# First attention of a two-layer block: the loads of stacks, values and output weight issued from ScalarE's queue in place of SyncE's

## The chip, the cores and the metric

One Trainium2 chip, one of its cores. The metric is the device time of one execution of the whole kernel in microseconds, the median of several executions. The core has TensorE (PE, matmuls), VectorE (DVE), ScalarE (ACT), GpSimd (POOL) and SyncE (SP); SP and ACT can both issue DMAs, each from a queue of its own. Each engine runs its own program in order and meets the others at semaphores.

## The reference, cut to what matters

Two transformer layers in fp32: x of 2 x 1024 x 512, each layer an attention and a feed forward, each wrapped as x + layernorm(f(layernorm(x))). The change concerns the first attention alone: 16 heads of width 32 per batch entry, rotary embedding, causal softmax.

```python
q, k, v = (proj(Wq), proj(Wk), proj(Wv))
q = q * cos + rotate_half(q) * sin
k = k * cos + rotate_half(k) * sin
scores = jnp.einsum('bhqd,bhkd->bhqk', q, k) / math.sqrt(HD)
scores = jnp.where(causal, -jnp.inf, scores)
attn = jax.nn.softmax(scores, axis=-1)
out = jnp.einsum('bhqk,bhkd->bhqd', attn, v)
```

## The kernel before, in words

The kernel runs phase after phase, with all engines meeting between them. `front_layer0` (before this phase) writes the rotated queries and keys of all heads, split into a high and a low part, and the values to DRAM. `attention_layer0` (L761) then works through 32 heads (16 per batch entry). For each head it holds

- a stack of queries and one of keys in SBUF, `q_stack` and `k_stack`, 96 rows by 1024 positions: the high part twice and the low part once against high, high and low, so that one matmul gives the product of the split numbers. Four such stacks (`STACKS`, L710) are kept in turn. `load_stack(h)` (L796) brings one in with four DMAs (L801 to L804);
- two more rows of the q stack, the negated maximum of every query's scores, in a high and a low part, against rows of ones in the k stack: the matmul of the scores then subtracts the maximum by itself. Those maxima are first computed from a matmul pass of their own;
- the values of a group of four heads (`GROUP_HEADS`), `v_stage`, 33 columns a head with a column of ones that gives the softmax sum. `load_values(group)` (L806) brings them in with one DMA (L811), two groups in turn.

The order of work is written out by `steps_layer0` (L733) as a sequence that every engine walks: i counts units, six to a head (`UNITS`: two for the first half of the queries, four for the second). At step i there is, in this order: at the first unit of a head the transpose of the next head's maxima ("N", L903, split by VectorE at L977 and L979); the scores of unit i + 2 ("Z", L912 on TensorE, exp at L940 on ScalarE); two of the twelve pieces of the maxima pass of the head two further on ("M", L893, reduced by VectorE at L968); the values product of unit i - 2 ("P", L928); and at two places of a head the output rows ("O") are copied out, on VectorE at L985 and, the softmax sums alone, on ScalarE at L946. The scores have two banks, so "Z" of a unit waits for the exp two units before it; ScalarE waits for the scores of the unit (L938), and for the first unit of a head TensorE waits for the maxima rows (L909).

SP issues every DMA of the phase, in this order. First stacks 0 and 1, values 0, stacks 2 and 3, values 1, and the output weight for the next phase (L844 to L850). Then, in step with the sequence: at unit 2 of a head the two DMAs that put the next head's maxima into its q stack (L855 to L858; they wait for VectorE's split); at unit 4 the stack four heads on (L861, once the scores of the head that held the slot are done), at the end of a group the values two groups on (L863), and the store of the softmax sums of the head before (L865, waits for ScalarE's copy). Some units later, once per group, the four heads' sums are loaded back in another layout (L869; it waits for the last two stores to have landed), inverted by VectorE (L957), stored (L871) and loaded broadcast (L873), and GpSimd multiplies the outputs by them (L1003). ScalarE issues no DMA.

```python
if k == 4 and 0 <= h and h + STACKS < HEADS:
    load_stack(h + STACKS)
if k == LAG + 2 and h >= 1 and (h - 1) % GROUP_HEADS == GROUP_HEADS - 1 and (h - 1) // GROUP_HEADS + 2 < GROUPS:
    load_values((h - 1) // GROUP_HEADS + 2)
```

Of the kernel before, what the change touches and what calls it, by code (L numbers as in the profile page):

```python
# [23 lines left out]
KT = D // P  # L24
# [8 lines left out]
NH = 16  # L33
HD0 = D // NH
# [41 lines left out]
def f32(ap):  # L76

    return ap.bitcast(F32)
# [628 lines left out]
HEADS = B * NH  # L707
GROUP_HEADS = 4
GROUPS = HEADS // GROUP_HEADS
STACKS = 4  # L710
LAG = 2
RING0 = LAG + 3
QW = 3 * HD0
KW = QW + 2
UNITS = [(0, (0, 1)), (0, (2, 3)), (1, (0, 1)), (1, (2, 3)), (1, (4, 5)), (1, (6, 7))]
U = len(UNITS)
# [5 lines left out]
def pieces(u):  # L722

    s, kts = UNITS[u]
    out, at = [], 0
    for kt in kts:
        c = max(0, kt - QT * s) * P
        out.append((kt, c, at, kt >= QT * s))
        at += SPAN - c
    return s, out, at  # L730

def steps_layer0():  # L733

    for i in range(FIRST, LAST):
        h, k = divmod(i, U)
        if k == 0 and 0 <= h + 1 < HEADS:
            yield "N", i, h + 1
        if 0 <= i + 2 < HEADS * U:
            yield "Z", i, i + 2  # L740
        if h + 2 < HEADS:
            yield "M", i, 2 * (h * U + 2 * U + k)
            yield "M", i, 2 * (h * U + 2 * U + k) + 1
        p, o = i - LAG, i - LAG - 1
        if 0 <= p < HEADS * U:
            yield "P", i, p
        if 0 <= o < HEADS * U and o % U in (1, U - 1):
            yield "O", i, 2 * (o // U) + (o % U == U - 1)
# [12 lines left out]
def attention_layer0(nc, m, ident, ident_bf, mask, qk_dram, v_dram, sums_dram, inverse_dram, out, next_load):  # L761
# [9 lines left out]
    q_stack, k_stack = (m.sb(n, [P, STACKS, S], F32R) for n in ("q_stack", "k_stack"))  # L771
    v_stage = m.sb("v_stage", [P, 2, TB, GROUP_HEADS, VW])
# [4 lines left out]
    stack_loaded = [m.sem(f"stack_loaded{i}") for i in range(STACKS)]  # L777
    v_loaded = [m.sem(f"v_loaded{i}") for i in range(2)]
    next_loaded = m.sem("next_loaded")
# [7 lines left out]
    scores_full, exp_done = m.sem("scores_full"), m.sem("exp_done")  # L787
    values_done = m.sem("values_done")
# [4 lines left out]
    with nc.Block() as block:  # L793
        @block.sync
        def _(sp):
            def load_stack(h):  # L796
                b, g, j = h // NH, h % NH // GROUP_HEADS, h % GROUP_HEADS
                slot, rows = h % STACKS, slice(j * HD0, (j + 1) * HD0)
                if h >= STACKS:
                    sp.wait_ge(scores_full, (h - STACKS + 1) * U)  # L800
                sp.dma_start(f32(q_stack[0:2 * HD0, slot, :]), qk_dram[b, 0, :, g, rows, :]).then_inc(stack_loaded[slot], 16)  # L801
                sp.dma_start(f32(q_stack[2 * HD0:QW, slot, :]), qk_dram[b, 0, 0, g, rows, :]).then_inc(stack_loaded[slot], 16)
                sp.dma_start(f32(k_stack[0:HD0, slot, :]), qk_dram[b, 1, 0, g, rows, :]).then_inc(stack_loaded[slot], 16)
                sp.dma_start(f32(k_stack[HD0:QW, slot, :]), qk_dram[b, 1, :, g, rows, :]).then_inc(stack_loaded[slot], 16)  # L804

            def load_values(group):  # L806
                b, g = divmod(group, KT)
                slot = group % 2
                if group >= 2:
                    sp.wait_ge(values_done, (group - 1) * GROUP_HEADS * U)  # L810
                sp.dma_start(v_stage[:, slot].rearrange("p t j c -> p t (j c)"),  # L811
                             v_dram[b, g].rearrange("t p c -> p t c")).then_inc(v_loaded[slot], 16)

            def store_sums(h):
                sp.wait_ge(sums_copied, 2 * h + 2)
                sp.dma_start(sums_dram[h:h + 1, :], sum_rows[HD0:VW, h % 2].rearrange("p s t -> p (s t)")
                             ).then_inc(sums_stored[h % 2], 16)

            def load_sums(group):
                last = group * GROUP_HEADS + GROUP_HEADS - 1  # L820
                for h in (last - 1, last):
                    sp.wait_ge(sums_stored[h % 2], 16 * (h // 2 + 1))
                rows = sums_dram[group * GROUP_HEADS:(group + 1) * GROUP_HEADS, :]
                if group >= 2:
                    sp.wait_ge(inverse_stored[group % 2], 16 * (group // 2))
                sp.dma_start(sums[:, group % 2, :], rows.rearrange("h (q c) -> (h q) c", c=GROUP_HEADS * S // P)
                             ).then_inc(sums_loaded[group % 2], 16)

            def store_inverse(group):
                sp.wait_ge(inverted, group + 1)  # L830
                rows = inverse_dram[group * GROUP_HEADS:(group + 1) * GROUP_HEADS, :]
                sp.dma_start(rows.rearrange("h (q c) -> (h q) c", c=GROUP_HEADS * S // P), sums[:, group % 2, :]
                             ).then_inc(inverse_stored[group % 2], 16)

            def load_inverse(group):
                sp.wait_ge(inverse_stored[group % 2], 16 * (group // 2 + 1))
                if group >= 2:
                    sp.wait_ge(scaled, 2 * (group - 1))
                for j in range(GROUP_HEADS):
                    sp.dma_start(inverse[j * HD0:(j + 1) * HD0, group % 2, :],  # L840
                                 inverse_dram[group * GROUP_HEADS + j, :].partition_broadcast(HD0)
                                 ).then_inc(inverse_loaded[group % 2], 16)

            load_stack(0)  # L844
            load_stack(1)
            load_values(0)
            load_stack(2)
            load_stack(3)
            load_values(1)
            sp.dma_start(*next_load).then_inc(next_loaded, 16)  # L850
            for i in range(FIRST, HEADS * U + 24):
                h, k = divmod(i, U)
                if k == 2 and 0 <= h + 1 < HEADS:
                    n = h + 1
                    sp.wait_ge(m_done, use["N", n] + 1)  # L855
                    sp.dma_start(f32(q_stack[QW:QW + 1, n % STACKS, :]), f32(negmax_hl[0:TB, n % 2, 0, :])
                                 ).then_inc(max_loaded[n % 2], 16)
                    sp.dma_start(f32(q_stack[QW + 1:KW, n % STACKS, :]), f32(negmax_hl[0:TB, n % 2, 1, :])  # L858
                                 ).then_inc(max_loaded[n % 2], 16)
                if k == 4 and 0 <= h and h + STACKS < HEADS:  # L860
                    load_stack(h + STACKS)  # L861
                if k == LAG + 2 and h >= 1 and (h - 1) % GROUP_HEADS == GROUP_HEADS - 1 and (h - 1) // GROUP_HEADS + 2 < GROUPS:
                    load_values((h - 1) // GROUP_HEADS + 2)  # L863
                if k == LAG + 2 and 0 <= h - 1 < HEADS:
                    store_sums(h - 1)  # L865
                group, late = divmod(i - (U * (GROUP_HEADS - 1) + 8 + LAG), U * GROUP_HEADS)
                if 0 <= group < GROUPS:
                    if late == 3:
                        load_sums(group)  # L869
                    elif late == 7:  # L870
                        store_inverse(group)  # L871
                    elif late == 10:
                        load_inverse(group)  # L873
            for group in range((HEADS * U + 23 - (U * (GROUP_HEADS - 1) + 8 + LAG) - 10) // (U * GROUP_HEADS) + 1, GROUPS):
                load_sums(group)
                store_inverse(group)
                load_inverse(group)
            sp.wait_ge(next_loaded, 16)

        @block.tensor  # L880
        def _(pe):
# [49 lines left out]

        @block.scalar
        def _(act):
            for kind, i, n in steps_layer0():
                if kind == "Z":
                    _, _, wide = pieces(n % U)
                    r = n % RING0
                    act.wait_ge(scores_full, n + 1)  # L938
                    wait(act, values_done, n - RING0 + 1)
                    nc.scalar.activation(probs[:, r, 0:wide], sbank[:, n % 2, 0:wide], ACT.Exp).then_inc(exp_done, 1)  # L940
                elif kind == "O":
                    h, s = divmod(n, 2)
                    act.wait_ge(values_done, h * U + (U if s else 2))
                    if s == 0 and h >= 2:
                        act.wait_ge(sums_stored[h % 2], 16 * (h // 2))
                    nc.scalar.copy(sum_rows[HD0:VW, h % 2, s, :], obank[HD0:VW, s, :]).then_inc(sums_copied, 1)  # L946

        @block.vector
        def _(dve):
# [1213 lines left out]
```

## Time and profile before

| | us |
|---|---|
| median of 3 executions | 3539.45 (3537.19 to 3541.39) |
| the profiled execution | 3529.51 |
| its span, first to last instruction | 3527.7 |
| the first attention within it | 196.5 to about 794 |
| TensorE busy over the span | 3004.4 (85%) |
| VectorE / ScalarE / GpSimd busy | 1879.8 / 1110.4 / 657.9 |
| mean granted TensorE clock | 0.929 |

The profile gives one execution in microseconds from its first instruction. A timeline row is: start, duration, engine, line of the kernel, operation, what it writes and what it reads, how many were merged; in brackets the idle time of the engine before it and what ended that. SPq is the queue side of SP: the duration of a DMA row there is how long its issue took, not the transfer. PEclk is the granted clock of TensorE, 1.00 for 2.4 GHz and 0.50 for 1.2 GHz.

### The profile page before, as it was taken

The page shows a single profiled execution, that of the slowest core. Times are in us where ns is not written, and L with a number is a line of the kernel's source. Part 1 is how long each engine was busy: PE and PEld are TensorE (multiplying, and loading weights), DVE is VectorE, ACT ScalarE, POOL GpSimd, SP SyncE. Part 2 cuts the span into 40 slices and gives each one's busy share as a digit, 9 for nine tenths or more (in the row PEclk, how much of TensorE's full clock was granted, in tenths as well). Part 3 has the DMA queues.
Part 4 walks back from the last instruction along what each step waited for, and adds up shares of the span by engine and source line. Part 5 has one row for each costly group of instructions (what it writes and reads, how often), then busy time and mean ns, then how long its engine had stood idle before and what let it go on. Part 6 is the DMA issues. An engine that isn't in the chain of part 4 may idle for free. (4 is left out here: it accounts for less than half of the span.)

```text
span 3527.7 us, 41847 instructions
## 1 busy us (share of the span) xinstructions
PE 3004.4 (85%) x14636; PEld 2258.6 (64%) x14636; DVE 1879.8 (53%) x3497; ACT 1110.4 (31%) x2215; POOL 657.9 (19%) x536
## 2 busy tenths in 40 slices
PE   8949999987899999556799999688999995388994
PEld 6824444435688888435688888576888883367773
DVE  5524454438223322435566666655666666667755
ACT  2213333333211111113344444233444442233331
POOL 1200000004111111302200000141000001266643
PEclk9959999998899999768999999899999996699997
DMA  4431222202200000374000000211000002210002
GB/s 142 133 114 56 65 63 65 68 28 96 72 18 19 18 18 1 112 279 171 26 32 21 31 21 31 78 75 37 21 31 31 21 27 95 72 36 28 8 1 95
DMA packets 111740, 207.82 MB, mean 59 GB/s; under 512 B 9376, under 2 KB 55456, under 8 KB 110848
## 3 DMA queue, kind: packets, MB, share of 16 engines
q1 hardware_dynamic: 111616, 206.21, 17.1%
q8 instruction: 73, 1.20, 0.1%
q14 instruction: 51, 0.42, 0.0%
HBM read 147.59 MB, written 58.33 MB: 58 GB/s over the span
## 5 line engine op out<-in xcount | busy, mean ns | idle before, releaser
L1238 PE MATMUL l1a_obank<-l1a_pT_hl,l1k_v_hl 128*128 128x512 f32 (+3 forms) x1152 | 300.2, 370 | 7.1 <-DVE l1a_pT_hl L1311 7.1
L1311 DVE TENSOR_TENSOR l1a_pT_hl<-l1a_work,l1a_pT_hl 128x512 fp32r<-128x512 f32 (+3 forms) x384 | 212.9, 555 | 154.1 <-ACT l1a_pT_hl L1271 153.9
L1218 PE MATMUL l1a_scores<-l1k_kT_hl,l1a_qa_hl 128*128 128x512 f32 (+3 forms) x1152 | 290.8, 361 | 1.5 <-ACT l1a_probs L1264 1.5
L928 PE MATMUL l0a_obank<-l0a_probs,l0a_v_stage 128*33 128x512 f32 (+3 forms) x768 | 290.4, 502 | 0.0
L1264 ACT ACTIVATE l1a_probs<-l1a_scores,l1a_row 128x128 f32<-128x128 f32 (+7 forms) x256 | 189.3, 741 | 317.2 <-DVE l1a_row L1301 317.2
L940 ACT ACTIVATE l0a_probs<-l0a_sbank 128x896 f32<-128x896 f32 (+1 forms) x192 | 155.5, 810 | 385.4 <-PE l0a_sbank L915 243.0
L968 DVE TENSOR_REDUCE l0a_halves<-l0a_mbank 128x1 f32<-128x512 f32 (+3 forms) x256 | 139.4, 586 | 178.9 <-PE l0a_mbank L893 178.8
L1246 PE MATMUL l1a_work<-l1a_wov,l1a_oT_hl 128*128 128x512 f32 x768 | 214.3, 402 | 5.0 <-DVE l1a_oT_hl L1330 3.0
L1271 ACT CAST l1a_pT_hl<-l1a_work 128x512 fp32r<-128x512 f32 (+3 forms) x384 | 183.6, 478 | 105.9 <-PE l1a_work L1229 104.6
L1643 DVE TENSOR_TENSOR f0f_hid<-f0f_silu,f0f_ubank 128x512 f32<-128x512 f32 x64 | 44.0, 688 | 321.5 <-PE f0f_ubank L1578 321.5
L1301 DVE TENSOR_REDUCE l1a_row<-l1a_scores 128x1 f32<-128x128 f32 (+7 forms) x256 | 189.7, 750 | 44.1 <-PE l1a_scores L1221 44.0
L1325 DVE SCALAR_TENSOR_TENSOR l_acc<-l1a_work,l1a_row,l_acc 128x512 f32<-128x512 f32 x256 | 189.4, 750 | 34.4 <-PE l1a_work L1246 25.5
L1218 PE MATMUL l1a_scores<-l1k_kpe,l1a_q_stack 128*128 128x512 f32 (+3 forms) x768 | 203.2, 346 | 0.0
L1218 PEld LDWEIGHTS l1a_scores<-l1k_kT_hl,l1a_qa_hl 128*128 128x128 f32 x1152 | 188.1, 190 | 21.7 <-ACT l1a_probs L1264 1.8
L1229 PE MATMUL l1a_work<-all_ident,l1a_probs 128*128 128x128 f32 x1152 | 191.8, 275 | 9.5 <-DVE l1a_qa_hl L1316 6.1
L1238 PEld LDWEIGHTS l1a_obank<-l1a_pT_hl,l1k_v_hl 128*128 128x128 f32 x1152 | 181.4, 191 | 28.9 <-DVE l1a_pT_hl L1311 14.9
L1354 POOL TENSOR_TENSOR l1a_q_stage<-l1k_qpe,l1a_ones 128x512 fp32r<-128x512 f32 x32 | 33.3, 1040 | 872.8 <-PE l1a_work L1246 816.9
L1578 PE MATMUL f0f_gbank<-x_xT,f0f_wT 128*128 128x512 f32 x768 | 192.5, 400 | 1.4 <-DVE f0f_wT L1637 1.4
L1588 PE MATMUL f0f_ybank<-f0f_wT,f0f_h_hl 128*128 128x512 f32 x768 | 189.9, 396 | 0.1
L1578 PE MATMUL f0f_ubank<-x_xT,f0f_wT 128*128 128x512 f32 x768 | 189.3, 395 | 0.0
L1588 PE MATMUL f1f_ybank<-f1f_wT,f1f_h_hl 128*128 128x512 f32 x512 | 139.9, 418 | 55.3 <-DVE f1f_h_hl L1647 36.3
L1698 POOL TENSOR_TENSOR f0f_h_hl<-f0f_hid,f0f_h_hl 128x512 fp32r<-128x512 f32 x64 | 82.7, 1292 | 477.6 <-ACT f0f_h_hl L1615 477.6
(249 smaller groups left out, 5806.3 us busy)
## 6 DMA issues: line engine op xcount, KB each, us to landing
qk_dram<-l0f_stage SPq DMA_DIRECT2D x8, 2048.0 KB, 8.5
l1a_wov<-wov_dram SPq DMA_DIRECT2D x32, 512.0 KB, 3.3
l1a_wabs<-wabs_dram SPq DMA_DIRECT2D x32, 384.0 KB, 3.8
l0a_q_stack<-qk_dram SPq DMA_DIRECT2D x32, 256.0 KB
l0a_k_stack<-qk_dram SPq DMA_DIRECT2D x32, 256.0 KB
wov_dram<-w1a_wov SPq DMA_DIRECT2D x16, 512.0 KB, 3.3
f1f_raw<-in_L_ffn_w_gate_up SPq DMA_DIRECT2D x16, 512.0 KB, 4.5
wabs_dram<-w1a_wabs SPq DMA_DIRECT2D x16, 384.0 KB, 2.4
```

The costliest lines, as they stand in the source:

```text
L928: last = pe.matmul(obank[0:VW, s, c:SPAN], v_stage[:, group % 2, kt, j, :], probs[:, r, at:at + SPAN - c], start=kt == 0, stop=kt == QT * ...
L1218: last = pe.matmul(scores[:, buf, cols], lhs, rhs, start=(i == 0), stop=(not diagonal and i == len(steps) - 1))
L1229: last = pe.transpose(work[:, slot, i * P:(i + 1) * P], probs[s][:, first + n, :], ident[:, :])
L1238: last = pe.matmul(obank[:, c:SPAN], src["v_hl"][:, a, n, :], pT_hl[:, ring(n, s), b, c:SPAN], start=(n == 0 and i == 0), stop=(n == QT * ...
L1246: last = pe.matmul(work[:, slot, :], oT_hl[:, s, a, n * P:(n + 1) * P], wov[:, hp, b, :], start=(i == 0), stop=(i == 2))
L1264: nc.scalar.activation(probs[s][:, first:first + wide, :].rearrange("p k c -> p (k c)"), scores[:, n % S_AHEAD, 0:wide * P], ACT.Exp, bias ...
L1271: nc.scalar.copy(pT_hl[:, ring(n, s), 0, c:SPAN], work[:, slot, c:SPAN]).then_inc(turned_high, 1)
L1301: nc.vector.tensor_reduce(row[:, 0, row_slot:row_slot + 1], scores[:, n % S_AHEAD, 0:wide * P], AX.X, ALU.max, negate=True).then_inc(max_d ...
L1311: nc.vector.tensor_tensor(pT_hl[:, r, 1, c:SPAN], work[:, slot, c:SPAN], f32(pT_hl[:, r, 0, c:SPAN]), ALU.subtract).then_inc(work_free[slo ...
L1325: nc.vector.scalar_tensor_tensor(out=out[:, t, :], in0=work[:, slot, :], scalar=row[:, 2, row_slot:row_slot + 1], in1=out[:, t, :], op0=AL ...
L1578: last = pe.matmul(bank[:, b, :], wT[:, half, wa, w, c * HG + b * P:c * HG + (b + 1) * P], xT_hl[:, xa, c, a * SPAN:(a + 1) * SPAN], start ...
L1588: last = pe.matmul(ybank[:, b % 2, :], h_hl[:, a % 2, ht, ha, b * P:(b + 1) * P], wT[:, half, wa, 2, ht * D:(ht + 1) * D], start=(n == 0), ...
```

## The change

`load_stack` and `load_values` move from SP's program into ACT's, and so do the loads at the start, the one of the output weight and the wait for it at the end. Two things differ beside the engine. At the start stack 2 is issued ahead of values 0. In the steady part ACT issues a stack right behind the exp of the last unit of a head (the waiting condition is the same), and the values behind the exp of the first unit of the next head. SP keeps the DMAs of the maxima, the sums and the inverses, in their old order.

```diff
@@ SP's program
-            load_stack(0)
-            load_stack(1)
-            load_values(0)
-            load_stack(2)
-            load_stack(3)
-            load_values(1)
-            sp.dma_start(*next_load).then_inc(next_loaded, 16)
             for i in range(FIRST, HEADS * U + 24):
...
-                if k == 4 and 0 <= h and h + STACKS < HEADS:
-                    load_stack(h + STACKS)
-                if k == LAG + 2 and h >= 1 and (h - 1) % GROUP_HEADS == GROUP_HEADS - 1 and (h - 1) // GROUP_HEADS + 2 < GROUPS:
-                    load_values((h - 1) // GROUP_HEADS + 2)
...
-            sp.wait_ge(next_loaded, 16)
@@ ACT's program
+            def load_stack(h):
...
+                if h >= STACKS:
+                    act.wait_ge(scores_full, (h - STACKS + 1) * U)
+                act.dma_start(f32(q_stack[0:2 * HD0, slot, :]), qk_dram[b, 0, :, g, rows, :]).then_inc(stack_loaded[slot], 16)
...
+            def load_values(group):
...
+                if group >= 2:
+                    act.wait_ge(values_done, (group - 1) * GROUP_HEADS * U)
+                act.dma_start(v_stage[:, slot].rearrange("p t j c -> p t (j c)"),
...
+            load_stack(0)
+            load_stack(1)
+            load_stack(2)
+            load_values(0)
+            load_stack(3)
+            load_values(1)
+            act.dma_start(*next_load).then_inc(next_loaded, 16)
             for kind, i, n in steps_layer0():
                 if kind == "Z":
...
                     nc.scalar.activation(probs[:, r, 0:wide], sbank[:, n % 2, 0:wide], ACT.Exp).then_inc(exp_done, 1)
+                    h, u = divmod(n, U)
+                    if u == U - 1 and h + STACKS < HEADS:
+                        load_stack(h + STACKS)
+                    group, rest = divmod(n - LAG - 4, U * GROUP_HEADS)
+                    if rest == 0 and 1 <= group and group + 1 < GROUPS:
+                        load_values(group + 1)
...
+            act.wait_ge(next_loaded, 16)
```

## Rows read from the trace of the kernel before

**Rows 1.** Busy time, granted clock (PEclk) and DMA of three stretches; us.

```profile
256.65:266.10 9.45, 9.45 (x26) 4.75 (x26) 3.41 (x8) 2.96 (x3) 0.00 (x0) 0.50 0.00 1
...
351.40:354.90 3.50, 3.50 (x7) 0.84 (x5) 1.65 (x4) 0.76 (x2) 0.00 (x0) 0.51 0.16 51
...
427.37:443.24 15.87, 15.79 (x65) 7.04 (x65) 8.31 (x18) 6.01 (x9) 2.50 (x2) 1.00 0.25 79
```

**Rows 2.** Waits of TensorE in 196 to 800 us and in 260 to 800: total, times, longest.

```profile
PE l0a_sbank L912 <- DMA l0a_q_stack<-l0a_negmax_hl: 38.2, 7, 23.8
...
PE l0a_sbank L912 <- DMA l0a_q_stack<-l0a_negmax_hl: 14.4, 6, 2.8
```

**Rows 3.** Timeline, start of the attention: SP's queue (SPq) and ACT; start, duration.

```profile
196.53 0.69 SPq L801 DMA_DIRECT2D l0a_q_stack<-qk_dram  x1
...
196.54 1.28 ACT L940 ACT_TABLE_LOAD   x1 [8.82 <-PEq L547]
...
208.61 9.76 SPq L801 DMA_DIRECT2D l0a_q_stack<-qk_dram  x1
...
232.56 9.70 SPq L850 DMA_DIRECT2D l_raw<-in_L_attn_Wo  x1
...
242.30 1.16 SPq L856 DMA_DIRECT2D l0a_q_stack<-l0a_negmax_hl  x1
```

**Rows 4.** Timeline, start of the attention: VectorE, TensorE and ScalarE.

```profile
222.02 0.28 DVE L979 TENSOR_TENSOR l0a_negmax_hl<-l0a_mbank,l0a_negmax_hl 8x128 fp32r<-8x128 f32 x1
...
251.26 0.80 PE L912 MATMUL l0a_sbank<-l0a_q_stack,l0a_k_stack 98*128 98x512 f32 x1 [23.78 <-DMA l0a_q_stack<-l0a_negmax_hl]
...
252.79 0.92 ACT L940 ACTIVATE l0a_probs<-l0a_sbank 128x896 f32<-128x896 f32 x1 [54.97 <-PE l0a_sbank L915]
...
256.68 1.20 PE L912 MATMUL l0a_sbank<-l0a_q_stack,l0a_k_stack 98*128 98x512 f32 x2
```

**Rows 5.** Timeline: SP's queue at heads 4, 6 and 29, TensorE at head 6.

```profile
306.55 0.68 SPq L856 DMA_DIRECT2D l0a_q_stack<-l0a_negmax_hl  x1
...
332.81 8.48 SPq L816 DMA_DIRECT2D sums_dram<-l0a_sum_rows  x1
...
347.22 0.67 SPq L856 DMA_DIRECT2D l0a_q_stack<-l0a_negmax_hl  x1
...
349.75 0.50 PE L912 MATMUL l0a_sbank<-l0a_q_stack,l0a_k_stack 98*128 98x512 f32 x1 [2.65 <-DMA l0a_q_stack<-l0a_negmax_hl]
...
725.33 0.67 SPq L856 DMA_DIRECT2D l0a_q_stack<-l0a_negmax_hl  x1
```

**Rows 6.** Timeline, ScalarE at the start of the next phases.

```profile
800.43 2.18 ACT L398 CAST l0o_ot_hl<-l_oT 128x512 fp32r<-128x512 f32 x4 [1.39 <-DVE l0o_eps L416]
...
802.63 1.28 ACT L392 ACT_TABLE_LOAD   x1
```

**Rows 7.** Timeline of a quiet head; last row: the tile's view, ns min/median/max.

```profile
437.04 0.92 ACT L940 ACTIVATE l0a_probs<-l0a_sbank 128x896 f32<-128x896 f32 x1 [1.57 <-PE l0a_sbank L915]
...
437.98 0.58 ACT L946 COPY l0a_sum_rows<-l0a_obank 1x512 f32<-1x512 f32 x1
...
439.98 0.49 ACT L940 ACTIVATE l0a_probs<-l0a_sbank 128x384 f32<-128x384 f32 x1 [1.43 <-PE l0a_sbank L915]
...
442.34 0.71 PE L912 MATMUL l0a_sbank<-l0a_q_stack,l0a_k_stack 98*128 98x512 f32 x2
...
445.28 0.72 PE L912 MATMUL l0a_sbank<-l0a_q_stack,l0a_k_stack 98*128 98x512 f32 x2
...
450.84 0.54 SPq L801 DMA_DIRECT2D l0a_q_stack<-qk_dram  x1
...
452.36 0.63 SPq L804 DMA_DIRECT2D l0a_k_stack<-qk_dram  x1
...
452.90 0.92 ACT L940 ACTIVATE l0a_probs<-l0a_sbank 128x896 f32<-128x896 f32 x1 [1.57 <-PE l0a_sbank L915]
...
L811 SPq DMA_DIRECT2D l0a_v_stage<-v_dram x8: 462/652/5502, 203.1 to 667.3; - x8
```

More of the change, by code:

```diff
@@ L795, in _ @@
         def _(sp):
[L796 to L812, printed above, removed]
             def store_sums(h):
@@ L933, in _ @@
         def _(act):
+            def load_stack(h):
+                b, g, j = h // NH, h % NH // GROUP_HEADS, h % GROUP_HEADS
+                slot, rows = h % STACKS, slice(j * HD0, (j + 1) * HD0)
+                if h >= STACKS:
+                    act.wait_ge(scores_full, (h - STACKS + 1) * U)
+                act.dma_start(f32(q_stack[0:2 * HD0, slot, :]), qk_dram[b, 0, :, g, rows, :]).then_inc(stack_loaded[slot], 16)
+                act.dma_start(f32(q_stack[2 * HD0:QW, slot, :]), qk_dram[b, 0, 0, g, rows, :]).then_inc(stack_loaded[slot], 16)
+                act.dma_start(f32(k_stack[0:HD0, slot, :]), qk_dram[b, 1, 0, g, rows, :]).then_inc(stack_loaded[slot], 16)
+                act.dma_start(f32(k_stack[HD0:QW, slot, :]), qk_dram[b, 1, :, g, rows, :]).then_inc(stack_loaded[slot], 16)
+            def load_values(group):
+                b, g = divmod(group, KT)
+                slot = group % 2
+                if group >= 2:
+                    act.wait_ge(values_done, (group - 1) * GROUP_HEADS * U)
+                act.dma_start(v_stage[:, slot].rearrange("p t j c -> p t (j c)"),
+                             v_dram[b, g].rearrange("t p c -> p t c")).then_inc(v_loaded[slot], 16)
+            load_stack(0)
[5 more added lines that the diff above has]
+            act.dma_start(*next_load).then_inc(next_loaded, 16)
             for kind, i, n in steps_layer0():
```

## The prediction

> **What bounds the kernel now.** I read the stretches first, then the waits, then the timeline at the start and at one group boundary, then SP's queue there. In a quiet head of the stage TensorE is busy 15.79 of 15.87 us at full clock, ScalarE only 6.01 [rows 1]: TensorE sets the pace of a head, and only what stops TensorE counts. The waits say what stops it: seven times the scores wait for the DMA that brings the maxima rows into the q stack, 38.2 us in all, one of them 23.8 us, the other six 14.4 us together [rows 2].
>
> The long one is at the start. The maxima of head 0 stand in SBUF at 222.3 us (222.02 + 0.28), but SP issues their DMA only at 242.30, because it first has to get 19 DMAs out (four stacks of four, two value loads, the output weight last). The queue takes issues no faster than the loads ahead of them drain: one stack issue holds SP 9.76 us, the weight's 9.70 us. TensorE starts on the scores at 251.26, the first exp runs at 252.79, and the third unit of scores, from which the work flows, begins at 256.68 [rows 3, 4].
>
> The six short ones repeat once per group of four heads. SP issues the next values, and its next DMA, the store of the sums, begun at 332.81, takes 8.48 us to issue. SP then has to see that store land before it may load the sums, and only then comes the maxima DMA, at 347.22; TensorE resumes at 349.75 after 2.65 us of idling [rows 5]. A quiet head gives 15.87 us from one maxima issue to the next [rows 1]. From the issue at 306.55 (head 4) to that at 725.33 (head 29) are 25 heads in 418.78 us; 25 x 15.87 is 396.75, so the six boundaries cost 22.0 us. The waits explain 14.4; the other 7.6 is the clock: behind four of the six waits it falls to 0.5 (1.2 GHz), as between 351.4 and 354.9 [rows 1], and TensorE does half the work there.
>
> **The change part by part.** (1) *Start, SP side.* SP now has nothing in its program ahead of the maxima of head 0. It can issue them at 222.3, two DMAs in 1.2 to 1.9 us. At the boundary the rows were usable at 349.75, 2.5 us after the first of the two was issued [rows 5], so here they are usable at 225 if the loads beside them don't matter. They do run beside the stacks. The Trainium skill (DMA: Bandwidth & Descriptors, Issuing engines are not separate DMA queues) says that queues of different engines still share the same DMA engines and interleave, so only issue time is saved; here the issue time was the 20 us. With a few us more they are in place when TensorE has done the maxima of head 1 (it stopped 23.8 us before 251.26, at 227.5 [rows 2, 4]). What TensorE did from 251.26 to 256.68, 5.4 us, the first two score units among it, is then done by about 233 and both score banks are full.
>
> (2) *Start, ACT side.* This is the new limit. ACT must issue all 19 DMAs before its first exp. The tail of the list is unchanged (stack 3, values 1, weight; only stack 2 and values 0 are exchanged), so I take SP's own time, 196.53 to 242.26 [rows 3]. The table load goes behind them: in the next phase it runs at 802.63, after the copies that precede its activation in the program and not at the head of the phase [rows 6]; so 1.28 us [rows 3] more, first exp at 243.6, end 244.5 (0.92 [rows 4]), and then the third unit of scores, at 244.6. Before it was 256.68: **gain 12.1 us**. The clock was 0.5 (1.2 GHz) in all of 256.65 to 266.10 with TensorE busy throughout [rows 1]; I let that stretch move with the work, unchanged. Bounds: if the clock rises one such stretch earlier because TensorE idles 12 us and not 24, up to 9.45/2 = 4.7 us more; if the maxima get through only when ACT has finished its issues, the scores start at about 246 instead of 251.3, a gain of 5. So 5 to 17.
>
> (3) *Group boundaries.* SP's store of the sums now follows the maxima and needs no turn behind stack and values; it is ready before them (the sum copies of the last head of a group lie two units ahead of the value load). Its 8.48 us of issue goes, the sums are loaded well before the next maxima are ready, and those go out when ready, two periods after 306.55, at 338.3 and not 347.22, 9 us earlier, against a stall of 2.65. What would be late next is nothing within 6 us. So the whole excess goes, and the falls of the clock behind it: **gain 22.0 us**. Bounds: 14.4 if the clock's falls had another reason, 22.0 at most.
>
> (4) *ACT pays for the issues.* Per head one stack load, four DMAs, 450.84 to 452.99 on SP: 2.15 us [rows 7]. On ACT it stands behind the last exp of the head, which waits for the same scores and so begins with it; the next exp begins at 452.90, 2.06 us later: it is pushed back by 0.1 us, or by 0.6 if the issue begins only when the last exp is through (0.49, as its like at 439.98). Who waits for that exp? The score unit two further on, for its bank. In the head before, the same exp ends at 437.96 and that unit starts at 442.34: 4.4 us of slack. Cost: nothing, 28 times; cover gone if the issues take over 2.06 + 4.4 = 6.4 us. Behind the next exp stand, once per group, the values, 0.65 us (median of eight; the 5.50 is at the start [rows 7]). The exp behind them starts 2.94 us after its predecessor (437.04, 439.98) and has 445.28 - 440.47 = 4.8 us until a score unit needs it; less the copy of the sums between them (0.58) and up to 0.6 us already lost, the values' issue may take 6.6 us. Cost: nothing, six times. ACT's next DMA is the next head's stack, a period less some 3 us later, so what held the sums' store for 8.48 us should find no one.
>
> (5) *Loads and their landing.* The stack leaves at the same condition as before (the last scores of the head in that slot), the values one unit later; both are needed heads later. Nothing. (6) *The tail* (the wait for the weight moves from SP to ACT, long landed; the sums of the last group were never behind a load): nothing.
>
> Sum: 12.1 + 22.0 = 34.1 us. Against the profiled execution: span 3527.7 to 3493.6, its time 3529.5 to 3495.4. The median of the runs shown, 3539.45, lies 9.9 us above that execution, in nothing this stage shows; so I predict 3539.45 - 34.1 = 3505.4 us. A measurement of this kernel tells about 0.2%, 7 us, from no change.
>
> **The rivals.** *A, the two queues get in each other's way at the start* (0.10): the maxima DMAs issue at 222.3 but are held while ACT's long issues are under way. Gain there 5 instead of 12, boundaries unhurt since their DMAs fall where no issue is long: 27 us, 3512. What speaks for it beyond the trace: the Trainium skill (Perfetto Trace Analysis, DMA Instruction — HWDGE) says that a DMA of this kind locks the descriptor generator for itself, and that the profiled time contains the wait for the lock. No row here shows two issuing engines.
>
> *B, the hold moves to ACT* (0.10): the values' issue, now on ACT, takes the 8.48 us that SP's store took behind it. Over by 8.5 - 6.6 = 1.9 us, six times 11.4, and with such gaps the clock falls again, up to 7.6: gain 34.1 - 19.0 = 15 us, 3524. Against: six times of eight the values' issue itself was short, only its follower was held.
>
> *C, nothing comes of it* (0.04): both rings drain through one place in order, the maxima still land behind all loads: 3539. Against: they were late in being issued, not in landing.
>
> *D, slower* (0.06): ACT's stack issues are held in the steady stretch as they were at the start, 9.76 us. Each then stops TensorE for 9.76 - 6.4 = 3.4 us, 28 times 94 us, less the 34: 3600. It decides from 6.4 + 34.1/28 = 7.6 us per stack load. For it: ACT is the one engine with work of its own between issues, and its exp feeds everything. Against: in the steady stretch SP issued a stack in 2.15 us, because the stack before had drained.
>
> **How the numbers follow.** Forecast 0.70, A 0.10, B 0.10, C 0.04, D 0.06. The predicted time is the first's. Low end: all of (2)'s upper bound, 34.1 + 4.7, and some scatter of the median: 3497. High end: B's 3524. That leaves out C, D and little else. Faster by over 0.2%: 0.90 (forecast, A, B); within: 0.04; slower: 0.06.
>
> **What the profile after would show.** Right: the first maxima issue near 222 to 224, TensorE on the first scores near 228, the first exp near 243.6 right behind the weight's issue and a table load on ACT, the third score unit near 245. No wait of the scores for the maxima DMA of over 0.5 us past 260, all maxima issues 15.87 us apart, and no fall of the clock between there and the stage's end. ACT's issues 2.2 us per stack. Wrong: score units idle on ACT's exp; a first maxima issue at 242 or one that lasts 10 us (A, C); a values issue of 8 us on ACT (B); stack issues over 6 us past the start (D). A first exp later than 246 or before 240 would make (2)'s term wrong in size.

## The result, and the profile after

| | before | after |
|---|---|---|
| median, us | 3538.32 (3533.61 to 3541.39, 4 executions) | 3495.55 (3493.46 to 3497.86, 4) |
| the profiled execution | 3529.51 | 3495.37 |
| its span | 3527.7 | 3493.6 |
| mean granted clock | 0.929 | 0.932 |

The ratio is 0.988, with a 95% interval of 0.9863 to 0.9898. The change makes the kernel faster by 42.8 us (1.2%) by these medians; the prediction said 3505.4, range 3497.0 to 3524.0. The measured median lies 1.45 us below the range. Span against span the gain is 34.1 us, the sum of parts to the tenth, and that is partly luck: the stage itself gave 32.6 us (598.24 to 565.64), and the other 1.5 us lie ahead of its first load (0.55) and behind it (0.95), where nothing was changed. The gap between 34.1 and 42.8 us is what the experiments have to explain.

The timeline after, at the start of the attention: the queue sides of ACT and SP, TensorE and ScalarE (start, duration, engine; answers to [rows 3, 4]).

```profile
195.98 1.09 ACTq L909 DMA_DIRECT2D l0a_q_stack<-qk_dram  x1
...
204.19 9.82 ACTq L910 DMA_DIRECT2D l0a_q_stack<-qk_dram  x1
...
215.65 15.08 ACTq L909 DMA_DIRECT2D l0a_q_stack<-qk_dram  x1
...
222.16 0.82 SPq L831 DMA_DIRECT2D l0a_q_stack<-l0a_negmax_hl  x1
...
228.10 0.78 PE L882 MATMUL l0a_sbank<-l0a_q_stack,l0a_k_stack 98*128 98x512 f32 x1
...
234.37 9.44 ACTq L928 DMA_DIRECT2D l_raw<-in_L_attn_Wo  x1
234.50 0.64 SPq L831 DMA_DIRECT2D l0a_q_stack<-l0a_negmax_hl  x1
...
243.84 1.28 ACT L935 ACT_TABLE_LOAD   x1 [56.70 <-issue]
245.13 1.30 ACT L935 ACTIVATE l0a_probs<-l0a_sbank 128x896 f32<-128x896 f32 x2
246.10 1.22 PE L882 MATMUL l0a_sbank<-l0a_q_stack,l0a_k_stack 98*128 98x512 f32 x2 [12.26 <-ACT l0a_probs L935]
```

The maxima of head 0 leave at 222.16, not 242.30, and TensorE goes from the maxima pass straight into the scores at 228.10. Then it stands still for 12.26 us, because ScalarE has its issues to finish: the weight's ends at 243.81, the table load follows, the first exp comes at 245.13. That ScalarE's issues set the start is as predicted.

The first group boundary after, queue sides and ScalarE (answers to [rows 5, 7]):

```profile
318.09 0.21 SPq L798 DMA_DIRECT2D sums_dram<-l0a_sum_rows  x1
319.34 0.37 SPq L808 DMA_DIRECT2D l0a_sums<-sums_dram  x1
327.43 0.64 SPq L831 DMA_DIRECT2D l0a_q_stack<-l0a_negmax_hl  x1
```

```profile
319.16 0.49 ACT L935 ACTIVATE l0a_probs<-l0a_sbank 128x384 f32<-128x384 f32 x1 [1.10 <-PE l0a_sbank L885]
319.17 0.50 ACTq L909 DMA_DIRECT2D l0a_q_stack<-qk_dram  x1
...
320.66 0.62 ACTq L912 DMA_DIRECT2D l0a_k_stack<-qk_dram  x1
321.39 0.92 ACT L935 ACTIVATE l0a_probs<-l0a_sbank 128x896 f32<-128x896 f32 x1 [1.73 <-PE l0a_sbank L885]
321.41 0.43 ACTq L919 DMA_DIRECT2D l0a_v_stage<-v_dram  x1
```

The store of the sums takes 0.21 us to issue where it took 8.48, and the maxima go out one period after the last ones. On ScalarE a DMA issue begins together with the exp ahead of it, and the exp behind waits for the issues: 321.39 - 319.16 = 2.23 us where it was 2.06 in the quiet head of before. The values' issue takes 0.43 us.

The windows view after: busy time (with counts), granted clock, DMA share, GB/s, in four stretches (answers to [rows 1]).

```profile
246.10:254.80 8.70, 8.70 (x23) 4.45 (x23) 2.86 (x6) 3.30 (x4) 0.00 (x0) 0.50 0.27 101
254.80:260.00 5.20, 5.20 (x23) 2.33 (x22) 2.76 (x5) 1.99 (x3) 0.00 (x0) 0.99 0.24 62
360.00:375.86 15.86, 15.78 (x66) 7.04 (x65) 8.31 (x18) 6.00 (x9) 0.00 (x0) 1.00 0.15 51
260.00:750.00 490.00, 486.42 (x1986) 214.75 (x1985) 246.81 (x510) 186.28 (x248) 17.55 (x14) 1.00 0.20 60
```

From 260 to 750 us the clock is full throughout, and a head takes 15.86 us as before (15.87). No wait for the maxima DMA is left in that stretch (they were 14.4 us, [rows 2]).

### The profile page after: what moved, and what is told of

It is laid out like the page before. It is cut to its first block and busy times, and to the rows that moved or that the text cites. A ratio compares the mean times of both kernels' runs of the same rounds, so it can differ in the third digit from the quotient of the medians.

```text
span 3493.6 us, 41847 instructions
## 1 busy us (share of the span) xinstructions
PE 2996.7 (86%) x14636; PEld 2256.8 (65%) x14636; DVE 1879.8 (54%) x3497; ACT 1110.8 (32%) x2215; POOL 658.7 (19%) x536
## 5 line engine op out<-in xcount | busy, mean ns | idle before, releaser
L1240 PEld LDWEIGHTS l1a_obank<-l1a_pT_hl,l1k_v_hl 128*128 128x128 f32 x1152 | 181.4, 191 | 28.8 <-DVE l1a_pT_hl L1313 14.8
L1356 POOL TENSOR_TENSOR l1a_q_stage<-l1k_qpe,l1a_ones 128x512 fp32r<-128x512 f32 x32 | 33.4, 1043 | 872.6 <-PE l1a_work L1248 816.7
```

The source lines that it names most:

```text
L1240: last = pe.matmul(obank[:, c:SPAN], src["v_hl"][:, a, n, :], pT_hl[:, ring(n, s), b, c:SPAN], start=(n == 0 and i == 0), stop=(n == QT * ...
```

## The experiments

Each run's trace gives the **stage**, from the first load's issue to the first transpose of the output weight in the next phase, and **the phases behind**, from there to the end of the span. Two such rows for the kernel before, run again (b1):

```profile
195.32 0.69 SPq L801 DMA_DIRECT2D l0a_q_stack<-qk_dram  x1
...
795.12 3.65 PE L132 MATMUL l0ot_bank<-all_ident,l_raw 128*128 128x128 f32 x16 [13.04 <-PEq L793]
```

| kernel | stage, us | phases behind, us | median, us (executions) | ratio to before, 95% |
|---|---|---|---|---|
| before, first trace | 598.2 | 2732.9 | | |
| before again, b1 | 599.8 | 2739.5 | 3532.48 (12) | 0.9998 (0.9983 to 1.0012) |
| e_start | 589.9 | 2733.7 | 3516.73 (12) | 0.9958 (0.9945 to 0.9971) |
| e_steady | 575.6 | 2736.5 | 3507.89 (6) | 0.9933 (0.9915 to 0.9952) |
| e_order | 579.0 | 2728.7 | 3508.23 (6) | 0.9944 (0.9924 to 0.9963) |
| after, first trace | 565.6 | 2732.0 | 3495.55 (4) | 0.988 (0.9863 to 0.9898) |
| after again, a1 | 563.0 | 2734.3 | 3496.65 (5) | 0.990 (0.9884 to 0.9916) |
| e_wide | 541.9 | 2730.6 | 3474.58 (4) | 0.9837 (0.9821 to 0.9853) |
| e_pad4 | 565.0 | 2735.1 | 3496.79 (2) | 0.9896 (0.9878 to 0.9915) |
| e_pad8 | 742.4 | 2735.7 | 3675.59 (1) | 1.040, no interval |

The runs b1, e_start, e_steady and e_order were compared with 23 executions of the kernel before (median 3530.79, 3518.71 to 3546.74), the runs a1, e_wide, e_pad4 and e_pad8 with 9 others (median 3533.30, 3525.74 to 3537.51). Two traces of one kernel differ by 1.6 us (before) and 2.6 us (changed) in the stage, so a difference of that size tells nothing.

**b1: the kernel before, unchanged.**

> The kernel before itself, run again with a profile. Theory 1 (its executions differ from one another because the clock falls behind a varying number of the six group waits): the spans differ by some 3 to 12 us and with them the time of the attention stage, and this trace has another set of clock falls between 260 and 780 us than the first one had (17.1 us at half clock); mean granted clock and time go together over the executions. Theory 2 (the 8.8 us between the profiled execution and the median lie elsewhere, in the phases behind): the stage takes 598.2 us again within 1 us, and the rest of the span takes the difference.

The stage took 599.8 us, 1.6 more than in the first trace, and the phases behind 6.6 more. The stretches at half clock (falls of the granted clock to 1.2 GHz) were other ones, as theory 1 wants: five between 340 and 695 us, 20.5 us in all, not four with 17.1. Two of them in the windows view:

```profile
349.20:352.60 3.40, 3.40 (x5) 0.51 (x3) 1.78 (x4) 0.89 (x2) 0.00 (x0) 0.50 0.16 55
482.30:489.10 6.80, 5.41 (x11) 1.92 (x11) 2.09 (x4) 1.49 (x2) 0.00 (x0) 0.50 0.22 70
```

But 3.4 us more at half clock is worth 1.7 us, not the 8.8 us between the first profiled execution and the median of 3538.32. Theory 1 accounts for a small part, and most of the difference lay behind the stage, as theory 2 says. Theory 2's "within 1 us" for the stage was missed by 0.6. The 23 executions of the kernel before spread over 28 us.

**e_start: only the start is ScalarE's.**

```diff
# after, with the steady loads back in SP's program
+                if k == 4 and 0 <= h and h + STACKS < HEADS:
+                    load_stack(h + STACKS)
...
                 if k == LAG + 2 and 0 <= h - 1 < HEADS:
                     store_sums(h - 1)
@@ ACT
-                    if u == U - 1 and h + STACKS < HEADS:
-                        load_stack(h + STACKS)
...
-                    if rest == 0 and 1 <= group and group + 1 < GROUPS:
-                        load_values(group + 1)
```

> Only the loads at the start, the output weight's among them, are issued from ScalarE; the loads of the steady stretch stay with SyncE. The sum of parts says 11 us under the kernel before (the third score unit at 246 instead of 256.7) with the six group waits as before, 22 us of excess. Theory 1: the executions scatter as those of the kernel before, by about 8 us, and the gain of the median is 11 as well. Theory 2: the same gain, so this run does not tell them apart but e_steady does.

The third score unit begins at 245.50. The boundary is that of before, down to the held store:

```profile
321.52 8.67 SPq L816 DMA_DIRECT2D sums_dram<-l0a_sum_rows  x1
335.24 0.35 SPq L826 DMA_DIRECT2D l0a_sums<-sums_dram  x1
335.64 0.67 SPq L849 DMA_DIRECT2D l0a_q_stack<-l0a_negmax_hl  x1
...
338.17 0.50 PE L904 MATMUL l0a_sbank<-l0a_q_stack,l0a_k_stack 98*128 98x512 f32 x1 [2.79 <-DMA l0a_q_stack<-l0a_negmax_hl]
```

The six waits sum to 14.3 us. The stage is 9.1 us under the mean of the two of before (599.0); the median is 14.8 us lower by the ratio (10 to 19), 11 expected. The third score unit comes 49.9 us after the first load's issue (245.50 - 195.58), where it was 60.2 and 61.3 us, so the start gained 10.2 to 11.4 us as expected. But between 334 and 700 us this trace has 23.9 us at half clock against 17.1 and 20.5, by half of the difference 1.7 to 3.4 us, an estimate, and that takes some of it back.

**e_steady: only the steady stretch is ScalarE's.**

```diff
# before, with the steady loads moved as in the change, the start left with SP
-                if k == 4 and 0 <= h and h + STACKS < HEADS:
-                    load_stack(h + STACKS)
...
@@ ACT
+                    if u == U - 1 and h + STACKS < HEADS:
+                        load_stack(h + STACKS)
```

> Only the loads of the steady stretch are issued from ScalarE; the start is SyncE's as before. The sum of parts says the first scores stay at 251 us and the group waits and the clock falls behind them go: 22 us in the traces. Theory 1: the median gains over 22, about 30 us, since the other executions of the kernel before lose more at the boundaries than the profiled one did, and the scatter falls to 4 us. Theory 2: 22 us and the scatter of before.

First exp at 252.74, as before. The windows view from 260 to 760 us:

```profile
260.00:760.00 500.00, 497.28 (x2020) 219.26 (x2019) 251.17 (x519) 189.48 (x253) 17.54 (x14) 0.99 0.20 60
```

No wait for the maxima DMA is left past 260, and TensorE idles 2.7 us in 500. Stage 575.6, 23.4 us less; by the ratio 23.7 us (17 to 30). The median's gain is nearer to theory 2's 22 us than to theory 1's 30, which lies at the very edge of the interval. The six executions still spread over 10.6 us, not theory 1's 4. Together with b1 that leaves little of theory 1. The two halves in stage time, 9.1 + 23.4 = 32.5 us, come within 0.9 to 3.5 us of the whole, which is 33.4 (565.6) or 36.0 (563.0).

**e_order: all loads stay with SyncE, one block moved up.**

```diff
+                if k == LAG + 2 and 0 <= h - 1 < HEADS:
+                    store_sums(h - 1)
                 if k == 4 and 0 <= h and h + STACKS < HEADS:
                     load_stack(h + STACKS)
...
-                if k == LAG + 2 and 0 <= h - 1 < HEADS:
-                    store_sums(h - 1)
```

> Everything stays with SyncE; the store of the sums alone is put ahead of the stack and value loads of the same unit. If it is the place in SyncE's order that costs the boundaries, and not SyncE's having loads at all, the maxima of the boundary head issue at about 341 to 343 instead of 347, the wait of 2.7 us goes or nearly so, and the time falls by 18 to 22 us in the trace (as much as e_steady). The rival, that the load of the sums now takes the 8.5 us of holding and the maxima stay late: under 5 us gained.

SP's queue at the first boundary:

```profile
327.96 0.23 SPq L816 DMA_DIRECT2D sums_dram<-l0a_sum_rows  x1
...
331.23 0.76 SPq L811 DMA_DIRECT2D l0a_v_stage<-v_dram  x1
332.10 7.97 SPq L826 DMA_DIRECT2D l0a_sums<-sums_dram  x1
340.12 0.67 SPq L856 DMA_DIRECT2D l0a_q_stack<-l0a_negmax_hl  x1
```

The DMA behind the values is held again, the load of the sums this time, for 7.97 us. But the store has landed meanwhile, so the second wait in the row is gone, and the maxima leave at 340.12. Five waits of TensorE are left, 2.1 us together. Stage 579.0, 20.0 us less than before; the median is 19.8 us lower by the ratio (13 to 27), 18 to 22 expected. So the boundaries' cost came from SP's order: a store whose landing SP must await was issued behind a load that holds the queue. Another engine isn't needed for 20 of the 23.4 us; of the other 3.4, the 2.1 us of waits can be seen, and the rest is within what two traces of one kernel differ by.

**a1: the changed kernel again.**

> The changed kernel once more, with more executions on both sides. Theory 2 (the attention stage gained the 33 to 34 us that the traces show, and the 9.9 us that the prediction added between the profiled execution and the median was chance in the phases behind): the ratio of the medians comes to 0.990 (34 us, 32 to 37), the stage takes 550 us from its first matmul to the transposes of the weight within 1 us, and the phases behind scatter between 2728 and 2740 us. The rival (the change is worth 42.8 us in most executions, which the traces miss): ratio 0.988 again.

Ratio 0.990 (0.9884 to 0.9916), 35 us of 3533; stage 563.0 and the phases behind 2734.3 us. The expected 32 to 37 us hold, and the 0.988 of the first comparison lies just outside this interval. (The 550 us of the expectation count from the first matmul; by that measure it is 758.40 - 209.49 = 548.9, 1.1 less.)

**e_wide: six DMAs to a stack.**

```diff
-                act.dma_start(f32(q_stack[0:2 * HD0, slot, :]), qk_dram[b, 0, :, g, rows, :]).then_inc(stack_loaded[slot], 16)
+                act.dma_start(f32(q_stack[0:HD0, slot, :]), qk_dram[b, 0, 0, g, rows, :]).then_inc(stack_loaded[slot], 16)
+                act.dma_start(f32(q_stack[HD0:2 * HD0, slot, :]), qk_dram[b, 0, 1, g, rows, :]).then_inc(stack_loaded[slot], 16)
...
-                act.dma_start(f32(k_stack[HD0:QW, slot, :]), qk_dram[b, 1, :, g, rows, :]).then_inc(stack_loaded[slot], 16)
+                act.dma_start(f32(k_stack[HD0:2 * HD0, slot, :]), qk_dram[b, 1, 0, g, rows, :]).then_inc(stack_loaded[slot], 16)
+                act.dma_start(f32(k_stack[2 * HD0:QW, slot, :]), qk_dram[b, 1, 1, g, rows, :]).then_inc(stack_loaded[slot], 16)
...
-                        pe.wait_ge(stack_loaded[hs], 64 * (h // STACKS + 1))
+                        pe.wait_ge(stack_loaded[hs], 96 * (h // STACKS + 1))
```

> The changed kernel with each stack brought in by six DMAs of 32 rows from one plane each, in place of four of which two gather 64 rows from two planes. Then here the first matmul comes about 10 us earlier (near 201 us), no issue at the start takes over 3 us, the first exp runs near 216 and the time falls by 25 to 30 us under the changed kernel. The rival (the start is bound by the amount of data, 5 MB in 54 us): under 5 us.

Its timeline at the start:

```profile
195.98 0.36 ACTq L909 DMA_DIRECT2D l0a_q_stack<-qk_dram  x1
...
201.82 0.45 PE L863 MATMUL l0a_mbank<-l0a_k_stack,l0a_q_stack 96*128 96x128 f32 x1 [15.40 <-DMA l0a_k_stack<-qk_dram]
...
204.38 1.26 ACTq L921 DMA_DIRECT2D l0a_v_stage<-v_dram  x1
...
209.15 0.60 ACTq L930 DMA_DIRECT2D l_raw<-in_L_attn_Wo  x1
209.78 1.28 ACT L937 ACT_TABLE_LOAD   x1 [22.64 <-issue]
212.39 0.82 SPq L831 DMA_DIRECT2D l0a_q_stack<-l0a_negmax_hl  x1
...
218.03 0.79 PE L882 MATMUL l0a_sbank<-l0a_q_stack,l0a_k_stack 98*128 98x512 f32 x1 [0.94 <-DMA l0a_q_stack<-l0a_negmax_hl]
...
219.56 0.92 ACT L937 ACTIVATE l0a_probs<-l0a_sbank 128x896 f32<-128x896 f32 x1 [8.49 <-PE l0a_sbank L885]
```

The start brings in the same bytes with eight more issues, and the long holds are gone: the longest issue at the start is 1.26 us, ScalarE is through at 209.75 and not 243.81, the first stack is in 5.8 us after its first issue and not 15.6. The third score unit begins at 223.45, 22.65 us earlier, and the stage is 22.4 us under the mean of the two of the changed kernel (564.3); the median is 22.1 us lower. I had expected 25 to 30: the first exp was put at 216, and it waits for the scores until 219.56, now behind TensorE's maxima pass. This kernel beats both, at 0.9837 of before. The rival, a start bound by the amount of data, falls: from 196 to 211 us the windows view gives the 16 DMA engines a busy share of 0.22 and 69 GB/s in the changed kernel, and 0.96 and 231 GB/s here. The Trainium skill (DMA: Bandwidth & Descriptors, Why a DMA increments its semaphore by 16 and not by 1) says that a DMA is spread over the largest number of engines up to 16 that divides the slowest dimension of both sides.
**e_pad4 and e_pad8: how much work ScalarE's cover holds.** The spare exps' results aren't used. Beside them and a semaphore that counts them, only a wait for the row of ones ahead of the first load is new.

```diff
                         load_stack(h + STACKS)
+                        for p in range(4):
+                            wait(act, padded, 4 * h + p)
+                            nc.scalar.activation(spare[:, :], ones[:, :].to_broadcast([P, 2 * SPAN]), ACT.Exp).then_inc(padded, 1)
```

> The changed kernel with four spare exps of 1024 columns (1.02 us each, results unused) on ScalarE behind every stack load of the steady stretch, 28 times. The prediction's slack says that 5.9 us of such work fit there (6.4 less the exp of 0.49): nothing lost, within the scatter. The rival (the issues have used up ScalarE's cover, and any more work behind them is paid in full): 28 x 4.1 = 115 us slower.

> The same with eight spare exps, 8.2 to 8.7 us. By the slack of 5.9 us each costs 2.3 to 2.8 us, 28 times: 64 to 78 us slower, and up to 48 us more where the clock falls behind such a gap (1.7 us each): 64 to 126 us. If nothing is lost the slack was counted too small; if 230 us are lost there was none.

With four, nothing is lost: 3496.79 (two executions), and the stage of 565.0 is that of the changed kernel. With eight the time is 3675.59 us (one execution), 179 us more than a1 and more than the 126 expected at most. Its timeline over one head:

```profile
410.28 0.49 ACT L938 ACTIVATE l0a_probs<-l0a_sbank 128x384 f32<-128x384 f32 x1 [1.10 <-PE l0a_sbank L887]
...
411.91 0.61 ACTq L914 DMA_DIRECT2D l0a_k_stack<-qk_dram  x1
...
412.57 8.66 ACT L944 ACTIVATE l0a_spare<-l0a_ones 128x1024 f32<-128x1024 f32 x8 [1.79 <-PE l0a_sbank L887]
...
421.14 0.90 ACT L938 ACTIVATE l0a_probs<-l0a_sbank 128x896 f32<-128x896 f32 x1
...
422.09 1.22 PE L884 MATMUL l0a_sbank<-l0a_q_stack,l0a_k_stack 98*128 98x512 f32 x2 [4.21 <-ACT l0a_probs L938]
```

The spare work begins at 412.57, when the four issues are through, not behind the exp of 0.49. I had taken the wrong one of the two from the 6.4 us. With the issues' 2.3 the room is 4.1 us: 8.66 - 4.1 = 4.5 us over, and TensorE waits 4.21. The four took 4.32 us and still fit, to within 0.2. Past the start the waits sum to 127.9 - 12.8 = 115 us over 28 heads. The other 64 us are what is left of the 179; they fit the granted clock, 0.87 in both stretches of 40 us here, where the changed kernel had 1.00:

```profile
400.00:440.00 40.00, 35.35 (x129) 15.46 (x129) 15.97 (x32) 24.28 (x29) 0.00 (x0) 0.87 0.11 35
440.00:480.00 40.00, 31.80 (x118) 14.06 (x116) 13.65 (x30) 24.38 (x29) 2.51 (x2) 0.87 0.22 61
```

So cover for the issues is there, and past 6.4 us per head it ends as sharply as rival D supposed, with the clock's part on top, which D had left out.

## Why the prediction was right or wrong

**The step that failed** is the last of the sum: "The median of the runs shown, 3539.45, lies 9.9 us above that execution, in nothing this stage shows; so I predict 3539.45 - 34.1". That put the whole 9.9 us into the changed kernel's median without a reason. Over 23 executions the kernel before has a median of 3530.79 and over 9 others 3533.30, so 1.3 to 3.8 us above the profiled 3529.51 and not 9.9; the three shown were high ones. The phases behind the stage, which no kernel here changed, took 2728.7 to 2739.5 us in ten traces, a spread of 10.8 us. So a difference of this size arises without anything in the stage, as the premise had it; where the three shown executions lost theirs can't be said, since they have no trace. Against the profiled execution the prediction gave 3495.4 us, and the medians were 3495.55 and 3496.65. The range was built from the terms of the stage, with "some scatter of the median" at its low end for 4 us; with a base known to 10 us it had to reach that much lower. How much of the first ratio (0.988) was chance can't be told exactly: the repetition gave 0.990, and the intervals overlap. Nor is it certain that chance alone made the three high: they begin at 3537.19, and of 44 later executions of the same kernel only 5 reached 3537 us. Another condition of the chip in those first runs stays open.

(1) *Start, SP side*: right. Issued at 222.16, scores from 228.10. Rival A did not happen: SP issued in 0.82 us while an issue of ScalarE's stood for 15.08 us, and in 0.64 beside one of 9.44. The Trainium skill's lock on the generator (Perfetto Trace Analysis, DMA Instruction — HWDGE) is thus not held against the other engine for as long as such an issue lasts; whether for a part of it, these rows don't tell.

(2) *Start, ACT side*: right in kind, 1.5 us off in size. The issues took 47.8 us (195.98 to 243.81) for the 45.7 of SP, and ended at 243.81 and not 242.26; the table load stood behind them, the third score unit began at 246.10: gain 10.6 for 12.1. On SP the long ones were 5.50, 9.76, 3.83, 5.11 and 9.70 us, here 9.82, 15.08 and 9.44; whether the exchange of stack 2 and values 0 made the difference was not tried by itself. The clock rose at 254.8 and not 266.1, 8.7 us behind that unit for 9.4.

(3) *Boundaries*: right. Over 25 heads, from 295.69 to 692.28, a head took 15.86 us in the mean, so the excess of 22.0 us is gone whole. e_steady shows 23.4 us by itself and e_order 20.0 without ScalarE. The 23.4 lie over the "22.0 at most"; they count from the mean of two traces, and from the one that the prediction read it is 22.6. The clock's part of it, 7.6 us, went with the waits.

(4) *ACT pays*: right, nothing. The exp behind the stack's issues came 0.17 us later (0.1 predicted), the values' issue took 0.43 us, and e_pad4 shows room for 4.3 us more. By e_pad8 the slack of 6.4 us was right to 0.3. Rivals B and D did not happen; e_pad8 shows what D would have cost.

(5), (6) Nothing moved there, as said. The end of the stage kept its wait of 12.9 us for the last group's inverses. C fell with the first row of SP.

## What to carry to other kernels

Look at what stands ahead of a small, urgent DMA on its queue: here a large load was cheap to issue itself and held the next issue for 8 to 15 us, and a store whose landing the engine itself awaits stood behind one. Reordering within the queue gave most of what the boundaries cost (20.0 of 23.4 us). For the start only the second queue was tried (9.1 us); an order on SP's queue that lets the first maxima out before the later loads was not. A second queue needs room on the engine that owns it, counted from the issue's start to the next result that is needed. Look also at why the loads hold the queue: giving them another form (e_wide) was worth another 22 us on top of moving them. And state a forecast against a base whose scatter is known: a median of three executions and a profiled one, 10 us apart, make a base known to 10 us, whatever the sum of the parts.

## What the hardware showed that I had not expected

- With two of its four DMAs gathering 64 rows from two planes, the first stack was usable 15.6 us after its first issue and the second 11.6 us later (211.58, 223.16). The same bytes as six DMAs of 32 rows from one plane were usable after 5.8 us.
- Two queues did not slow one another's issue: 0.82 us on SP within a 15.08 us hold on ACT.
- An activation behind DMA issues on ScalarE waits until the issues are through (the issues end at 412.52, the spare exps begin at 412.57), while the one ahead of them runs beside them (319.16 and 319.17).
- Idle gaps of some 4.2 us on TensorE in 28 heads came with another 64 us at a lower granted clock: 115 us of waits, 179 us of time (e_pad8, one execution).
